# SyncE issues the query and key loads of the next pair of sequences in front of this pair's masked-query loads

## The reference

```python
h = _layernorm(x, ln1_g, ln1_b)
qkv = h @ w_qkv + b_qkv
q, k, v = jnp.split(qkv, 3, axis=-1)
...
scores = jnp.einsum('bqhd,bkhd->bhqk', q, k) / np.sqrt(DK)
attn = jax.nn.softmax(scores, axis=-1)
o = jnp.einsum('bhqk,bkhd->bqhd', attn, v).reshape(B, S, D)
x = x + o @ w_o + b_o
h = _layernorm(x, ln2_g, ln2_b).reshape(B * S, D)
logits = h @ gate_w + gate_b
topv, topi = jax.lax.top_k(logits, TOPK)
```

## Time and profile before

| what | value |
| --- | --- |
| median of 3 runs | 771.48 us (765.51, 771.48, 772.9) |
| profiled execution, its own time | 765.54 us |
| its span | 763.7 us |
| mean granted clock of TensorE in it | 0.912 |
| PE / DVE / ACT / POOL busy in the span | 600.0 / 480.4 / 384.6 / 449.0 us |
| `qp` and `kp` loads | 48 + 48, 128 KB each, from SP |
| `qm` loads | 192, 32 KB each, from SP |

### The profile page before, as it was taken

The page is one execution under the profiler, slowest core; times in us unless marked ns, Lnnn a source line. Parts: engine busy times, 40 slices in busy tenths (PEclk is TensorE's granted clock), DMA queues, the critical chain, the costliest instruction groups (busy, mean ns, idle before and its releaser), DMA issues. The chain is left out here.

```text
span 763.7 us, 18100 instructions
## 1 busy us (share of the span) xinstructions
PE 600.0 (79%) x5634; PEld 483.7 (63%) x5634; DVE 480.4 (63%) x1470; ACT 384.6 (50%) x828; POOL 449.0 (59%) x588
## 2 busy tenths in 40 slices
PE   2999935999991767559899989999960699999950
PEld 1566625988991544327666666666740699999950
DVE  2555544766672699655557657656734487878835
ACT  1543403655560334246777777778640365555620
POOL 2477761766677556193545777777666056666650
PEclk9999976999995799959999999999975699999985
DMA  5921155777763168635454563564414988888519
GB/s 162 273 60 49 49 105 153 209 195 205 210 188 113 50 204 220 236 60 88 80 110 71 102 130 81 109 120 93 89 40 99 298 271 242 255 245 253 156 49 317
DMA packets 97833, 115.24 MB, mean 151 GB/s; under 512 B 16128, under 2 KB 77600, under 8 KB 97632
## 3 DMA queue, kind: packets, MB, share of 16 engines
q1 hardware_dynamic: 82224, 92.36, 46.9%
q0 software_dynamic: 9088, 18.76, 7.7%
q10 hardware_dynamic: 6448, 3.20, 1.8%
HBM read 80.75 MB, written 33.53 MB: 150 GB/s over the span
## 5 line engine op out<-in xcount | busy, mean ns | idle before, releaser
L472 POOL DMA_INDIRECT dispatch_rows<-row,index x128 | 128.1, 1000 | 62.4 <-issue 33.9
L1577 DVE TENSOR_REDUCE mneg<-ps 128x4 f32<-128x512 f32 x128 | 87.6, 687 | 77.1 <-PE ps L1711 76.9
L833 POOL DMA_INDIRECT expert_rows<-fo,to x78 | 84.0, 1077 | 68.4 <-DVE fo L1884 55.0
L833 POOL DMA_INDIRECT expert_rows<-eo,to x78 | 74.8, 959 | 50.0 <-ACT eo L926 28.1
L1662 ACT ACTIVATE prob<-ps 128x512 f32<-128x512 f32 x128 | 75.7, 592 | 40.8 <-PE ps L1723 40.3
L806 DVE CAST xh<-psT 128x256 fp32r<-128x256 f32 x78 | 33.1, 425 | 75.6 <-PE psT L774 75.0
L1655 ACT ACTIVATE km<-kp,const 96x512 fp32r<-96x512 f32 x96 | 68.1, 717 | 21.6 <-DMA kp<-qk_parts 10.6
L1711 PE MATMUL ps<-km,qp 96*128 96x512 f32 x128 | 63.7, 504 | 16.7 <-POOL km L1515 11.6
L1873 PE MATMUL psO<-wb,fh 128*128 128x128 f32 x624 | 75.9, 275 | 0.0
L1515 POOL TENSOR_SCALAR km<-kp,const 96x512 fp32r<-96x512 f32 x32 | 54.5, 1702 | 34.9 <-DMA kp<-qk_parts 21.7
L824 PE MATMUL psA<-xh,wh 128*128 128x256 f32 (+1 forms) x234 | 73.5, 314 | 0.0
(11 more groups left out here) (201 smaller groups left out, 1520.7 us busy)
## 6 DMA issues: line engine op xcount, KB each, us to landing
wb<-in_W1b SPq DMA_DIRECT2D x39, 578.0 KB
w<-in_W SPq DMA_DIRECT2D x39, 304.0 KB
qk_parts<-qk SPq DMA_DIRECT2D x8, 1024.0 KB, 5.0
qp<-qk_parts SPq DMA_DIRECT2D x48, 128.0 KB
kp<-qk_parts SPq DMA_DIRECT2D x48, 128.0 KB
qm<-qk_parts SPq DMA_DIRECT2D x192, 32.0 KB
xs<-dispatch_rows SPq DMA_DIRECT2D x39, 130.0 KB
xt<-dispatch_rows SPq DMA_DIRECT2D x39, 130.0 KB
```

Source lines behind the costliest of these rows:

```text
L472: pool.indirect_dma_start(out=m.xbuf, out_offset=bass.IndirectOffsetOnAxis(ap=r.index[b][:, c:c + 1], axis=0), in_=r.row[b][:, c // TOPK, ...
L833: pool.indirect_dma_start(out=m.ybuf, out_offset=bass.IndirectOffsetOnAxis(ap=to[b][:, a:a + 1], axis=0), in_=out[b][:, a, :], in_offset=N ...
L1577: nc.vector.tensor_reduce(mneg[s % 2][:, g, :], ps1[:, g % 2, :].rearrange("p (j k) -> p j k", j=4), AX_X, ALU.max, negate=True).then_inc( ...
```

## The change

The wait for the free buffer and the six loads of a pair are moved one iteration ahead: in iteration k, SP now loads pair k+1, in front of the wait and the twelve `qm` loads of pair k. For k = 0 nothing is loaded, since pairs 0 and 1 come from pre-attention; for k = 1 pair 2 is loaded with no wait; for k = 14 pair 15, the last. The value that the wait asks for is 8 x (ahead - 2) = 8 x (k - 1), the same as that of the `qm` wait behind it.

```diff
                 for k in range(PAIRS):
-                    if k >= 2:
-                        if k >= PAIR_BUFFERS:
-                            sp.wait_ge(shifted, HG * 2 * (k - PAIR_BUFFERS + 1))
-                        load_pair(m, sp, k, k % PAIR_BUFFERS)
+                    ahead = k + 1
+                    if 2 <= ahead < PAIRS:
+                        if ahead >= PAIR_BUFFERS:
+                            sp.wait_ge(shifted, HG * 2 * (ahead - PAIR_BUFFERS + 1))
+                        load_pair(m, sp, ahead, ahead % PAIR_BUFFERS)
                     if k < 2:
                         sp.wait_ge(zeroed[k], 1)
                     else:
```

## The result

| | before | after |
| --- | --- | --- |
| median of six runs each | 770.08 us (765.51 to 775.62) | 758.49 us (754.69 to 762.59) |
| profiled execution, its span | 763.7 us | 760.2 us |

The ratio is 0.9872, with a 95% interval of 0.983 to 0.9914: 9.9 us less of 770.08, between 6.6 and 13.1. The forecast was 765.5 us, 5.95 less. (The two medians of the table lie 11.6 us apart; the text goes by the ratio and its interval.) So the direction holds, and the gain is larger than forecast; 758.49 lies on the lower bound of the range, 758.5, and the nearest of the cases is the first rival ("more comes back", 759.6).

What follows compares the result with a forecast made beforehand. The prediction took late pair loads, queued behind `qm` issues, to lengthen attention laps where ACT waits; their excesses, 1.88 + 1.14 + 0.59 + 2.34 = 5.95 us, came off the median 771.48, giving 765.5 us, range 758.5 to 770.5.

Steps and rivals of the forecast that it cites:

- first rival: Pair waits in seven laps of the attention stage cost another 5.94 us in the median execution; 759.6 us, chance 0.17.
- What delays the pair loads is only their place behind twelve `qm` issues: SyncE's queue, attention stage: the buffer wait is already passed, so moving ahead issues the pair 4.1 us sooner.
- Sum of what pair loads cost today: 5.95 us: Attention laps 3, 5, 7 and 8 to 27: excess over similar laps, 1.88 + 1.14 + 0.59 + 2.34 us.
- T: Moment SyncE passes its wait for pair k: end of the shifts of pair k-2, end of lap 2k-3.
- ACT asks for pair 3 at T+8.7: ACT's mask in lap 3: the pair lands by T+8.1, before it is wanted, so ACT no longer waits.
- Cost 0: Later `qm` issue, by 2.7 us: it still lands by T+12.2, before its first shift, margin 1.0 to some 3 us.
- Sum: Closing total: 5.95 us taken from the profiled execution (759.6 us) and equally from the median 771.48, giving 765.5 us.
- third rival: First shift of each even lap: PE waits for late `qm`; 1 us late in pairs 2 to 15 gives 779.5, chance 0.05.
- one us per us and pair: Price in even laps if `qm` lands past its need: each us late costs one us for each pair.
- T+13.2: First shift of lap 4, for pair 2: when `qm` is wanted; landing later would make PE wait.

Runs made afterwards that it cites:

- the marks: Kernels before and after, each with waits and 32-byte DMAs added on SyncE to date the landings of `qm` and pair loads; 836.92 and 829.84 us.

## Why the prediction was right or wrong

- "What delays the pair loads is only their place behind twelve `qm` issues": right. In the three unmarked traces of the kernel after ACT never waits for `kp`, and POOL at most once, 0.4 us.
- "Sum of what pair loads cost today: 5.95 us": right for the execution it was read from. The lap totals of the first two profiles differ by 5.94.
- ACT asks for pair 3 at T+8.7, and the pair lands at T+7.1 to T+8.1 or a bit sooner: right, with the marks each pair had landed by T+6.9 to T+8.4, and ACT never waited.
- "Cost 0" for the later `qm`: right; it lands at T+9.3 to T+11.2, so the batch doesn't end later. The rule of the Trainium skill weighed there ("DMA: Bandwidth & Descriptors", section "Queues, rings and completion order": descriptors of a ring are taken in order) would put `qm` behind the whole pair, and the marks show `qm` landing after the pair each time; whether the order also protects the pair stays open.
- The term that came out too small is in "Sum": "The waits are a matter of lap order, not of one execution, so I take the same 5.95 from the median." The profile read was of an execution of 765.54 us, as fast as the fastest of the six before (765.51). In four more traces the kernel before pays 5.4 to 9.7 us over the kernel after, 7.6 in the mean; this is in line with the 8.1 and 9.1 us measured on those chips, though their intervals are too wide to rule out 5.95. For the first chip, 9.9 us (6.6 to 13.1) stand against one pair of traces with 5.94; that its other executions paid more in the same way is inferred from the other chips, not shown. Scatter in the other stages isn't ruled out as a part of it.
- That the measured time still lies at the edge of the range is owed to the first rival, which had a chance of 0.17. Its second 5.94 us was a guess from how far one execution lay from the median, so the nearness of its 759.6 to 758.49 is luck in the number.
- The first rival had the kind of the error right (landings differ, and the excess with them), and the argument against it, "the rest of the kernel has far more traffic", didn't hold on the other chips. Of the two traces that paid 9.7 us, each lost 1.6 us in a way that no rival named: a lap with 3.4 us at half clock, behind a lap with a late pair.
- The third rival's price, "one us per us and pair", was too low: 1.7 with `qm` late by some 3 us. Its place, the first shift of even laps, and its threshold, T+13.2, were right.

## What to carry to other kernels

When two groups of loads share a queue, issue first what is wanted first, and judge a wait by laps of the same kind with and without it, not by its sum. A wait whose length is a race between a landing and a lap varies from execution to execution: one profile gives one draw, and the time of the execution doesn't tell which: two executions of 836.91 and 836.92 us (the second with marks) had lap totals of 216.16 and 211.96. Take several traces, or give the cost a range. Before moving a load back, find its slack; here the load that was moved behind had 2.8 us left, issuing it 3 to 5 us later still cost 4.8 us though nobody waited for it, and issuing it six shifts later (7 us for the first pair) cost 80.

## What the runs showed of the hardware

- TensorE's granted clock fell to 0.50 (1.2 GHz) behind an idle of 4.2 us in the kernel with late `qm`, and for some 3.4 us in one lap each of two traces of the kernel before, right behind a lap with a late pair in which PE was idle for 1.5 and 1.8 us in all. It was back at 1.00 right after those 3.4 us. With late `qm` 46.3 us of waiting became 80.8 us of time, of which 29.4 are PE busy for longer with the same matmuls.
- Six loads of 128 KB, alone on the queue, land 5.3 to 6.8 us after the first issue, of which the issues take 2.7; the same six behind twelve of 32 KB take 5.7 to 8.1 where an engine waited for them.
- The same program took 765 to 776 us on one chip and 831 to 849 on two others (the kernel before), and on these the laps of the kernel after were nearly the same (206.5 against 204.4 us). The 70 us are in other stages; where exactly wasn't followed.
